# GNN kernel: in the first gather stage, TensorE selects one tile of each pair of groups from the fifth pair on

## The reference, cut to what matters

```python
W_rel = jnp.einsum('rb,bdf->rdf', w_comp, weight)
agg = jax.ops.segment_sum(h[src] * norm, etype * n_nodes + dst, ...)
node_repr = jnp.einsum('rnd,rdf->nf', agg.reshape(...), W_rel) + h_bias + h @ loop_weight
x = layernorm(x + relu(node_repr))
```

```python
e = (x_dst - x_src) @ theta_w.T + x_src @ phi_w.T
e = relu(bn(relu(bn(e)) @ fc1_w.T)); agg = segment_sum(e, dst)
x = layernorm(x + relu(agg / max(cnt, 1) + x))
```

## Time and profile before

| | us |
|---|---|
| median of 3 runs | 2509.78 (2509.06 to 2510.79) |
| the profiled execution, its own time | 2509.12 |
| its span in the trace | 2507.3 |
| busy: PE / DVE / POOL / ACT | 2085.5 / 1524.3 / 1542.6 / 692.1 |
| first gather stage: first to last gather | 11.03 to 992.38 |
| second gather stage: first to last gather | 1037.5 to 1930.1 |

### The profile page before, as it was taken

The page is one execution under the profiler, slowest core; times in us unless marked ns, Lnnn a source line. Parts: engine busy times, 40 slices in busy tenths (PEclk is TensorE's granted clock), DMA queues, the critical chain, the costliest instruction groups (busy, mean ns, idle before and its releaser), DMA issues. The chain is left out here.

```text
span 2507.3 us, 47644 instructions
## 1 busy us (share of the span) xinstructions
PE 2085.5 (83%) x13270; PEld 1635.5 (65%) x13271; DVE 1524.3 (61%) x3250; ACT 692.1 (28%) x1175; POOL 1542.6 (62%) x1693
## 2 busy tenths in 40 slices
PE   4777767767777677659999999999997998999997
PEld 4666666766667666635566666655564444999995
DVE  5443343334443433777778777777686887777776
ACT  3211111111111111642221222122212774434444
POOL 6777777777777776377777777777777001940002
PEclk9988888888888889858999999999998999999998
DMA  5222222222222221564434444444444983344342
GB/s 111 74 64 72 64 73 72 64 72 64 73 64 72 71 62 47 160 191 135 156 130 157 149 138 150 136 154 133 130 156 139 332 305 109 135 151 148 137 149 85
DMA packets 133160, 306.27 MB, mean 122 GB/s; under 512 B 34875, under 2 KB 83812, under 8 KB 115296
## 3 DMA queue, kind: packets, MB, share of 16 engines
q1 hardware_dynamic: 77040, 155.43, 18.9%
q0 software_dynamic: 47936, 98.17, 15.1%
q10 hardware_dynamic: 8112, 51.91, 5.1%
HBM read 241.95 MB, written 63.42 MB: 122 GB/s over the span
## 5 line engine op out<-in xcount | busy, mean ns | idle before, releaser
L781 POOL DMA_INDIRECT G<-in_x,srcT x782 | 744.2, 952 | 246.3 <-issue 180.1
L796 POOL DMA_INDIRECT G<-btab,srcT x716 | 675.5, 944 | 262.2 <-issue 164.9
L880 PE MATMUL PS<-BIG,G 128*128 128x192 f32 x1564 | 356.2, 380 | 260.6 <-PEq L36 253.1
L880 PEld LDWEIGHTS PS<-BIG,G 128*128 128x128 f32 x1564 | 298.2, 220 | 291.7 <-issue 291.2
L1005 PE MATMUL PS<-BIG,ACC 128*128 128x384 bf16 x2112 | 364.3, 328 | 18.2 <-PEq L36 18.2
L1158 ACT ACTIVATE BIG<-PS 128x768 f32<-128x768 f32 x196 | 158.5, 809 | 786.3 <-ACTq L36 786.3
L1475 DVE TENSOR_TENSOR ACC<-ACC,PS 128x24 f32 x782 | 140.8, 180 | 321.2 <-DVEq L36 230.4
L1686 DVE TENSOR_SCALAR BIG<-typ_i 128x1920 bf16<-128x1920 bf16 x220 | 250.7, 1148 | 129.9 <-DVEq L36 127.6
L891 PE MATMUL PS<-BIG 128*128 128x192 f32 (+1 forms) x1584 | 328.8, 369 | 0.5 <-PEq L36 0.5
L891 PEld LDWEIGHTS PS<-BIG 128*128 128x128 f32 x1584 | 318.3, 226 | 0.6 <-issue 0.6
L1005 PEld LDWEIGHTS PS<-BIG,ACC 128*128 128x128 bf16 x2112 | 199.3, 98 | 144.9 <-issue 23.5
(11 more groups left out here) (204 smaller groups left out, 2298.9 us busy)
## 6 DMA issues: line engine op xcount, KB each, us to landing
BIG<-spill SPq DMA_DIRECT2D x90, 1024.0 KB, 4.8
spill<-BIG ACTq DMA_DIRECT2D x49, 1024.0 KB
BIG<-rel_d SPq DMA_DIRECT2D x49, 322.5 KB
G<-in_x,srcT POOLq DMA_INDIRECT x782, 2.5
typ_i<-in_edge_type SPq DMA_DIRECT2D x97, 128.0 KB
BIG<-atab SPq DMA_DIRECT2D x196, 60.0 KB
G<-btab,srcT POOLq DMA_INDIRECT x716
atab<-BIG SPq DMA_DIRECT2D x12, 384.0 KB, 2.9
```

The lines of the kernel that those rows point to most:

```text
L781: nc.gpsimd.indirect_dma_start(out=G[0:n, g % 2, t, :], out_offset=None, in_=x, in_offset=bass.IndirectOffsetOnAxis(ap=srcT[0:n, TPG * g + ...
L796: nc.gpsimd.indirect_dma_start(out=G[0:n, g % 2, t, :], out_offset=None, in_=btab[:, :], in_offset=bass.IndirectOffsetOnAxis(ap=srcT[0:n, ...
L880: mm = pe.matmul(PS[:, 2 * c + q // 2, (q % 2) * ZW:(q % 2 + 1) * ZW], G[:, h, TPC * k + q, :], soh[:, p, TPC * c + q, :, :].rearrange("p ...
```

## The change

From the fifth pair on (`FIRST_XPICK = 4`, pairs 4 to 23), the last tile of each pair's last chunk is not gathered. It is selected on PE from a table of x in SBUF.

- **Table.** `big_xtab` and `tab_more` hold x in three bf16 parts. In groups 0 to 6, two units of four windows a group are loaded by SP (`load_xunit`), split by ACT (`xunit_high`, `xunit_mid`) and DVE (`xunit_rest`, `xunit_low`). The room comes from `coef`, which now holds two pairs' coefficients in place of all.
- **Selection.** DVE's `xpick_hots` compares 128 indices with five windows (128x640, bf16 to bf16) 10 times a pair. PE's `sum_xpicks` has the one-hot as the stationary operand and the table as the moving one: 147 matmuls of 128 columns a pair, 120 of them in the even group, 27 in the odd. ACT copies the result into `G` (`put_xpicks`) and prepares the next pair's indices (`code_xpicks`, 5 ACTIVATEs of 128x128), for which PE spreads the two rows of digits (`spread_xpicks`).
- **Moved.** `split_picks` and `store_picks` go from the second stage into the first. `turn_nodes` stands at the head of each group and takes `seg_free` in place of `loop_done`; `loop_product` and the basis product behind it write the same bank and are one step for DVE, which adds the loop's product right behind the tiles. Four pairs are unrolled in place of one.

POOL's queue, first gather stage: before, then with the change.

The diff's core:

```diff
+    FIRST_XPICK = 4
-        coef = part(NC * TPC * TPR * B).rearrange("p (t k) -> p t k", k=B)
+        coef = part(2 * TPC * TPR * B).rearrange("p (t k) -> p t k", k=B)
+        big_xtab = part(ACC_UNITS * WPB * 3 * D // 2).bitcast(BF16).rearrange(...)
@@ SP
             def first_pass(g, h, use):
+                for p in range(2):
+                    u = xunit_of(g, p)
+                    if u is not None and u >= 2:
+                        load_xunit(u)
+                if isinstance(g, int) and g == 5:
+                    store_picks()
+                if prepares(g, h, use, FIRST_XPICK):
+                    load_xpick(use + 1)
                 take(sp, xw_free)
@@ POOL
-                        for q in real_tiles(g, k):
+                        for q in (range(TPC - 1) if xpicks(g, g % 2, g // 2, k) else real_tiles(g, k)):
@@ PE
+            def sum_xpicks(batches):
+                for b in batches:
+                    take(pe, xpick_oh_ready)
+                    for w in range(BATCH * b, min(BATCH * (b + 1), NW)):
+                        for a in range(3):
+                            mm = pe.matmul(xpicked, xpick_oh[:, BATCH * (b % 2) + w % BATCH, :], xtable_part(w, a), ...)
+                    mm.then_inc(xpick_oh_free, 1)
+
+            def finish_xpicks(g, h, use):
+                if picking(g, h, use, FIRST_XPICK) and h == 1:
+                    sum_xpicks((8, 9))
+                    if prepares(g, h, use, FIRST_XPICK):
+                        spread_xpicks()
...
+                    turn_nodes()
                         scaled_sums(g, h, use, 0)
-                        if not (isinstance(g, int) and g == 0):
-                            basis_product(1, False)
-                        turn_nodes()
-                        scaled_sums(g, h, use, 1)
+                        if xpicking and h == 0:
+                            sum_xpicks((0, 1))
+                        if not wide_tiles:
+                            finish_xpicks(g, h, use)
+                        loop_product()
+                        if xpicking and h == 0:
+                            sum_xpicks((2, 3))
+                        scaled_sums(g, h, use, 1, put=not wide_tiles)
+                        if xpicking and h == 0:
+                            sum_xpicks((4, 5))
                         basis_product(0, h == 0)
-                        loop_product()
-                by_pairs(pe, NG, one)
+                        if xpicking and h == 0:
+                            sum_xpicks((6, 7))
+                by_pairs(pe, NG, one, head=FIRST_XPICK, tail=1)
@@ ACT
+                if putting:
+                    take(act, xpick_spread_done)
+                    put_xpicks()
+                take(act, xwT_ps)
+                act.sem_inc(xw_free, 1)
+                act.activation(XT[:, bass.ds(g * TNODES, TNODES)], x_turned, ACT.Copy).then_inc(xwT_ready, 1)
+                if coding and putting:
+                    code_xpicks()
@@ DVE
+                    if xpicking:
+                        xpick_hots((2, 3) if p == 0 else (6, 7))
                     if not first:
                         starts = firsts_of(dve, before, TPP)
-                        take(dve, seg_ready)
+                    take(dve, seg_ready)
+                    if u is not None:
+                        xunit_rest(u)
...
+                    if p == 0:
+                        add_loop(g)
+                    dve.sem_inc(seg_free, 1)
+                    if u is not None:
+                        xunit_low(u)
+                    if xpicking:
+                        xpick_hots((4, 5) if p == 0 else (8, 9))
+                    if prepares(g, h, use, FIRST_XPICK) and p == 1:
+                        take(dve, xpick_code_ready)
+                        xpick_hots((0, 1))
```

More of the change, by code:

```diff
@@ L204, in gnn_kernel @@
         relx = part(CHUNK)[0:WIN, :]
-        pick_hi, pick_rows = (part(PICK // 2).bitcast(BF16) for _ in range(2))
+        pick_rows = part(PICK // 2).bitcast(BF16)
         at[0] = 2 * GROUP + CPG * CHUNK + GROUP
@@ L875, in scaled_sums @@
                     k = 2 * p + c
-                    reached(pe, "pe", x_gathered[CPG * h + k], gathered(g, k, use))
+                    reached(pe, "pe", x_gathered[CPG * h + k], x_landed(g, h, use, k))
+                    if put and xpicks(g, h, use, k):
+                        take(pe, xpick_put)
                     if copied:
@@ L886, in basis_product @@
                 bank = 4 + (1 - quarter if quarter is not None else p)
-                take(pe, seg_free)
+                if bank == 4 or quarter is not None:
+                    take(pe, seg_free)
                 if coef_too:
@@ L1159, in copy_z @@
                                    PS[:, 2 * c:2 * c + banks, 0:2 * ZW], ACT.Copy).then_inc(z_copied, 1)
-                    if k == (0 if last(g, NG) else 2):
-                        take(act, xwT_ps)
-                        act.sem_inc(xw_free, 1)
-                        act.activation(XT[:, bass.ds(g * TNODES, TNODES)], PS[:, 7, 0:P], ACT.Copy).then_inc(xwT_ready, 1)
-            by_pairs(act, NG, copy_z)
+                    if u is not None and c == 1:
+                        xunit_mid(u)
+                if coding and not putting:
+                    take(act, xpick_spread_done)
+                    code_xpicks()
+            by_pairs(act, NG, copy_z, head=FIRST_XPICK, tail=1)
             def deviations0(u):
```

227 lines of the change are left out of this document (155 added, 72 removed).

## The result

| | before | after |
|---|---|---|
| median, us | 2510.28 (2509.06 to 2510.82, 4 runs) | 2495.24 (2493.38 to 2496.63, 4 runs) |
| ratio, with its 95% interval | | 0.9943 (0.9931 to 0.9955) |
| the profiled execution | 2509.12 | 2493.38 |
| its span | 2507.3 | 2491.5 |
| first gather stage: first to last gather | 11.0 to 992.4 | 11.1 to 973.2 |

The change makes the kernel faster by 15.0 us in the medians and 15.7 in the profiled executions. The prediction said 25.0, and a range up to 2493; the time lies 2.2 us above that range.

A forecast was written before the change was run, and what follows sets the result against it. POOL's issue of gathers, one each 1.25 us, was taken as the bound; 20 fewer take 25.0 us off 2509.78, other work hidden at zero cost: 2484.8 us (2484.1 for the profiled execution), range 2479 to 2493 (0.81).

The forecast's parts named there:

- The gathers taken away: POOL, first gather stage: one gather fewer in each of pairs 4 to 23, 20 x 1.25 = 25.0 us, all on the path.
- the 967 of the prediction: First gather stage: the last of 762 gathers at about 967 us in place of 992.4.
- PE's pair of 35.9 us: PE, first stage: 25.5 + 8.8 + 1.6 = 35.9 us a pair, hidden behind POOL's 38.8 with 2.9 us left.
- the hand-off: Odd group: PE waits for two ACT copies and three steps between engines before the loop's product, 1.3 us.
- The price of a matmul: PE's selection: 60 ns for each bf16 matmul of 128 columns, 147 making 8.8 us a pair.
- DVE: First stage: ten added comparisons at 0.53 us and gaps make 7.8 us, 26.6 of 38.8 us a pair.
- The table and the moved steps: Groups 0 to 6: PE starts up to 5 us later, POOL doesn't see it; cost zero, at most 3.
- The first rival: First stage: DVE's new comparisons slow POOL's gathers by 21 us, time 2506; chance 0.06.
- The fourth rival: End of first stage: PE at full clock shortens it, time 2479 to 2482; chance 0.05.
- The second rival: First stage: PE's pair lasts a little longer than POOL's 38.8 us, time 2488 to 2505; chance 0.11.
- The range: Whole kernel: 2479 to 2493 us, holding the forecast, the fourth rival and part of the second rival; chance 0.81.
- The sign to look for: POOL, first stage: waits for `g_free` over 0.3 us would show the prediction wrong, PE's pair being too long.

The follow-up runs named there:

- the kernel before with the same rows: Kernel before the change, types' comparison in two calls of 5 and 3 tiles, output rows 130 elements apart: 2505.23 us, ratio 0.9985.
- the selection with one part: Changed kernel with PE's selection cut to the table's high part, 49 matmuls a pair in place of 147: 2490.60 us, ratio 0.9922.
- the kernel with the fill: Changed kernel plus 100 bf16 matmuls into unread PSUM in the first stage's last group, no other edit: 2495.47 us, ratio 0.9928.

## Why the prediction was wrong, point by point

- **The gathers taken away, 20 x 1.25 = 25.0 us: right.** 762 gathers, 160 in 200 us in the steady part. With the late loads and the hold removed the last one comes at 966.2. That this is near the 967 of the prediction is in part luck: 967 still held the old comparison's 3.4 us, and the edit took that away as well; against the kernel before with the same rows it is 22.6 us.
- **PE's pair of 35.9 us: right as a sum, and in part by luck.** In groups 8 to 13, where PE was late and only its work and its turns with DVE and ACT set its pace, a pair took 35.4 us. One of these pairs, and PE's waits in all three (218 to 324 us):

```profile
253.20:288.90 35.70, 32.22 (x310) 30.71 (x309) 20.44 (x56) 8.37 (x16) 27.11 (x29) 1.00 0.27 70
```

```profile
PE PS L936 <- PEq L36: 4.9, 4, 1.4
PE PS L1003 <- PEq L36: 2.9, 3, 1.0
PE PS L961 <- PEq L36: 2.4, 3, 1.1
PE PS L936 <- ACT BIG L1291: 1.0, 1, 1.0
```

  PE was busy 31.6 us a pair, where the sum had 34.3: bursts that follow each other at once overlap at their ends, so two chunks in a row took 2.77 and not 2 x 1.54. It stood still for 3.7 us a pair, where the sum had 1.6 with the spreading matmul: the hand-off was 0.97 for 1.3, and two waits, ahead of a chunk (up to 1.4) and ahead of the first selection (1.1; the text foresaw "1 to 2 us" there), were not in the sum. The two errors cancel. The price of a matmul was right:

```profile
271.41 1.91 PE L961 MATMUL PS<-BIG 128*128 128x128 bf16 x30 [1.08 <-PEq L36]
```

  (1.91 - 0.16) / 30 = 58 ns each for the 60 taken. By the 81 ns of the Trainium skill ("TensorE: Matmul & The Clock Gate", Back-to-back issue gap) the burst would have been 2.6 us, and PE, at 39.0 us a pair for POOL's 38.8, would not have caught up, by an estimate from that figure; here the trace doesn't agree with it. The rows of the selection with one part above show the slack. This was the term that I was least sure of.
- **DVE: right.** The new comparison is 0.486 us (0.53), and no gather beside it is longer than usual.
- **The table and the moved steps, "Cost zero, at most 3": the step that failed.** The text saw that SP's load of x stands behind a unit's load and that "PE starts a group up to 5 us later", and set this to zero "being allowed 40 us". That took the allowance as full. It isn't: at the start of the stage POOL is ahead of PE by nearly all of it (the text itself found 3.9 us left in one place), and it is given back only in the groups behind, in which PE is faster than POOL. Before, PE's groups took 10.0, 13.4, 14.3 and 15.5 us for POOL's 20 and the lag was gone by group 4. With the change they took 15.7, 21.9, 23.9, 20.9 and 22.2, and the lag stayed between 29 and 37 us in groups 0 to 6, until PE's late start at 151 us, with the store of the digits as one more step on SP ahead of it, put POOL to waiting. The price was 2.8 us in the first trace and about 4 in the medians, near the "at most 3", and the forecast took zero.
- **What was not priced at all: the old comparison's place.** The first rival asked whether the *new* comparisons hold the gathers, rightly said no, and took the old one's 3.4 us as given. Its price depends on where in POOL's step of 1.25 us it begins, and the change moved that: 3.0 us more between the two traces. What moved it, the new instructions on DVE's queue or PE's new pace behind which DVE works, was not taken apart. I had the rows for this in hand: 1.02 in the earlier trace rows against a longest of 1.317.
- **What was turned around: the stage's end.** The fourth rival hoped that a higher clock would shorten it. In the steady part the clock did rise, 0.84 to 0.97. But the last group, with no selection in it, has PE idle as before, and the low stretch fell on the only chunks that can't hide it: 2.9 us in the profiled execution, and not shown in the median.
- **The second rival,** PE's pair a little over POOL's, gives about the time that was measured (2495), and for the wrong reason.
- **The range** reached 8 us up, for one cost at a time. Three costs of 3 us, each taken as nothing or left out, add up to 8.7 of the 9.3 us by which the profiled execution missed its 2484.1, and left it. Two of them are shown by edits, the third only in traces.

The sign to look for that the prediction named, waits of POOL for `g_free` over 0.3 us, did come; its reading there, "then PE's pair is too long", was wrong. They came at 155 and 158 us, and the first new comparison of a selection ran at 199.9.

## What to carry to other kernels

A buffer's depth is slack only as far as it isn't already in use: follow the lag between the producer and the consumer through the stage's first groups, and count each new delay against what is left there, not against the depth. When instructions are put into a kernel, ask also which old ones move; one that collides with the bound's engine may cost more at its new place with no change to itself. Load what the next group starts with ahead of what only fills a table.

## What the runs showed of the hardware

- **A comparison of int32 to bf16, 128x1024, holds an indirect gather's issue on POOL,** as a `tensor_scalar` (0.75 us) and as a `tensor_tensor` with both inputs in SBUF (1.225). A gather that starts inside it is longer by what is left of it, less some 0.12 us: 0.44 with 0.56 left, and 0.90 with 1.03 left in the rows above. A `tensor_scalar` that begins up to 0.5 us inside a gather holds that one too, until 0.12 us behind its own end; the `tensor_tensor` didn't (no gather longer in all such cases of two traces). It goes the other way too: where the `tensor_scalar` begins 0.47 to 0.7 us inside a gather, or up to 0.1 us ahead of one, it is the comparison that takes longer, up to 0.985 us for 0.752.
- **The same comparison on rows at a pitch of 130 elements,** in two calls, holds nothing: the longest gather after the first 165 us was 957 to 962 ns in the four kernels that had it. It costs 1.49 us of DVE for 0.75. bf16 to bf16 with such rows on the input side holds nothing either: no gather took over 0.961 us in the second stage beside L1686, and none over 0.962 in the first stage beside L1638 once the types' comparison let them through. Whether the pitch or the shorter call is what counts was not tried by itself.
- **Selection by one-hots on PE** at 128 columns, bf16, each matmul with its own weights, ran at 58 ns each in bursts of 30 at 2.4 GHz.
- **PE's granted clock fell to the lower level, 1.2 GHz,** at the end of the stage (0.52 in 972 to 979 us) around an idle stretch of 3.66 us, and a chunk's sums took 2.90 us for 1.54; in the kernel with the fill they took 1.52 there.
- **An indirect gather of 128 rows** took 0.944 or 0.947 us in the median, by the execution and in both stages alike, with 0.30 us to the next.
